# Relative products of pair 0 and loads of pairs 0 to 3 moved into layer 0's experts, router logits by token tile, part of layer 1's weight split moved into the softmax stage

## The chip, the cores and the metric

The kernel runs on one core of a Trainium2 chip. The metric is device time in microseconds (us), as the median of three runs. Engines are called PE (TensorE, matmul), PEld (its weight load), DVE (VectorE), ACT (ScalarE), POOL (GpSimd) and SP (SyncE). SPq and POOLq are the queues from which SP and POOL issue DMAs.

## The reference

Two transformer layers over x of shape (2, 1024, 128), 2048 tokens. Each layer is

```
xn = layernorm(x)
x  = x + attention(xn) + mixture_of_experts(xn)
```

- Layer 0, attention: 16 heads of 8, Q, K and V are xn with signs, probabilities are a causal sigmoid of the scores (no row maximum).
- Layer 0, experts: 32 experts of width 64, the top 4 of a softmax router with group limits, and a shared expert of width 128. In the kernel all experts are computed for all tokens and weighted, most weights being zero.
- Layer 1, attention: q, k, v and output projections, softmax, 16 heads of 8, and a relative term: the score of query i and key j has an added product of q_i with one of 256 position vectors, chosen by the offset of j from i and constant outside a band.
- Layer 1, experts: 16 experts of width 176, the top 4 of a sigmoid router, and a shared expert of width 352, weighted likewise.

## The kernel before

Everything is one program of five stages, each a block with a body for every engine. An engine runs its body in the order written; all engines meet between two blocks. Semaphores written by hand order the rest.

1. `prepare` and `sigmoid_attention` (to 210 us): layer 0's attention, with the split of layer 0's expert weights beside it.
2. `experts` with k = 0 (212 to 403 us). Matrix products in this kernel are three matmuls each: an operand is a high part (`_hi`, rounded) and a low part (`_lo`, the rest), and hi x hi, lo x hi and hi x lo are summed. The 2048 tokens are 4 tiles `ti` of 512 columns, the hidden rows 17 chunks of 128, so K = 17 and M = 68 steps n. In step n, PE does `rise(n)` (gate and up products, 6 matmuls) and `fall(n-2)` (down product, 3 matmuls); ACT the silu and the high part of the hidden chunk; DVE the product with gate, then with `share`, the expert weights of each token (L1499); POOL the low part. The tile `share` has four slots (WB = 4): in its step n, SP waits until the hidden chunk n-4 is done and issues the loads of share n (L234, one per expert in the chunk, so two as a rule).
   After the last chunk of a tile, its finish follows in the steps behind it, beside the next tile's chunks: `after(n)` gives the tile and the offset o. At o = 3 to 13 the tile is turned, added to x and normalized, at 13 to 14 turned back and split, at 16, 18 and 20 PE makes q, k and v of layer 1. All these go through one PSUM bank, `z_ps`, so that each waits until the one before is copied out: q is split at o = 17, k at 19, v is saved at 21. SP stores q (three DMAs, L1198) at o = 21 and k (six DMAs, `ka` and `kb`, L1203) at o = 23. For the last tile the same offsets run behind the last chunk (TAIL = 24).
3. `softmax_attention` (403 to 932 us): 16 pairs of heads, each with 16 slots. `scores(m)` (L885) gives the scores from which DVE takes row maxima; LS = 14 slots later `turned(n)` (L898) computes them again with keys on the partitions, for the exponential (L977), and `values` multiplies them with v (L925). The relative products `offsets(r)` (L872), 384 wide, are saved by ACT (L973), stored by SP with a padded row to DRAM (L773) and read back skewed (L786), two to a read; DVE adds them in the band (L1022), PE in the turned scores (L910). They lead by LR = 26 slots, so that the stage opens with 12 slots in which only relative products are made; there they use the free PSUM banks and DVE helps to save them (L1010). The loads of pair 0 are SP's (L762), those of pairs 1 to 3 POOL's (L816), behind the fills of `qs`, `ka` and `kb` (L800, L990, L991). At the stage's start PE computes the router's logits for all 16 token tiles (L931 to L933); DVE's `choose` picks experts between slots. Every eight slots PE turns the eight columns of row maxima (L956), DVE copies them (L1042), and SP stores them into `qs`. Behind the last slot the router's weights are turned (L279), copied by ACT (L288) and stored by SP (L294). POOL stores every finished half pair of the output (L826).
4. `experts` with k = 1 (932 to 1193 us): the same loop with K = 25 and M = 100. No weights are ready; groups of three chunks are loaded by SP into `raw` (L1159, L1162), split by ACT (L1327) and POOL (L1231) while the first tile runs. Before the loop SP also loads the attention output and its sums, `xn` and `v`, 1 MB each (L1187).

Of the kernel before, what the change touches and what calls it, by code (L numbers as in the profile page):

```python
# [54 lines left out]
LO_ROW = 64  # L55
SHARES = 4
# [40 lines left out]
def choose(router, sb, dve, then, chosen, part):  # L97
# [80 lines left out]
    else:  # L178
# [8 lines left out]
        dve.tensor_tensor(cw[:, :, 0:E], hot[:, 0], view(rs[:, 1, :], [1, NT], [0, E]), ALU.mult).then_inc(router.cw_ready, 1)  # L187

# [258 lines left out]
def sigmoid_attention(nc, d, sb, scr, router, weights, y_stored):  # L447
# [7 lines left out]
    KEPT = 10  # L455
    HELD, LAG = 9, 4
    TURN, STEP = 20, 6 * P
    UPPER, LOWER = (0, 7, 1, 6, 2, 5, 3, 4), (0, 3, 1, 2)
    with ExitStack() as ctx:
# [6 lines left out]
        qs, ks = tile("q", [P, 2, T], F32R), tile("k", [P, 2, T], F32R)  # L466
# [196 lines left out]
def softmax_attention(nc, d, sb, scr, router, weights, y_stored, table):  # L663
# [3 lines left out]
    KEYROWS = 31  # L667
# [7 lines left out]
    KEPT = 6  # L675
    VALUES = (2, 1, 0, 2, 0, 2, 0, 1, 1, 2, 1, 0, 2, 0, 2, 0)
    KEYS = ((5, 0, 1, 6, 2, 7, 3, 4), (4, 0, 3, 5, 1, 6, 2, 7))
    with ExitStack() as ctx:
# [31 lines left out]
        rel_ready, saved_act, saved_dve = sem("rel_ready"), sem("saved_act"), sem("saved_dve")  # L710
# [8 lines left out]
        def rows(pair, hd, count):  # L719
            g = 2 * (pair % 2) + hd  # L720
            return slice(32 * g, 32 * g + count)
# [4 lines left out]
        LEAD = LR - LS  # L726

        def on_act(r):
            return r >= LEAD or r % 2 == 0

        def rel_bank(r):
            if r >= LEAD or r % 5 == 0:
                return rel_ps
            return duo[1 + r % 5 // 3][:, r % 5 % 2 * CH:(r % 5 % 2 + 1) * CH]

        def saved_before(r):
            return sum(on_act(x) for x in range(r)), sum(not on_act(x) for x in range(r))

        slots = range(-LR, SLOTS + 4)
        job_of = {}  # L740
        for n in slots:
# [107 lines left out]
        def _(pe):  # L849
# [86 lines left out]
            for n in slots:  # L936
# [3 lines left out]
                if r < SLOTS:  # L940
                    offsets(r)
# [696 lines left out]
```

## Time and profile before

| what | value |
|---|---|
| three runs | 1195.48, 1197.96, 1201.27 us |
| median | 1197.96 us |
| profiled execution | 1194.37 us |
| its span, first to last instruction | 1192.6 us |
| busy, share of the span | PE 86%, PEld 54%, DVE 63%, ACT 61%, POOL 45% |
| mean granted clock of PE | 0.947 of full speed |
| DMA | 197.42 MB, mean 166 GB/s |

The profile is one execution. The busy shares are means over stages that differ; where PE is not busy at nine tenths or more, the page's slices and the windows show it. Times within the profile count from the start of the span.

### The profile page before, as it was taken

The page shows a single profiled execution, that of the slowest core. Times are in us where ns is not written, and L with a number is a line of the kernel's source. Part 1 is how long each engine was busy: PE and PEld are TensorE (multiplying, and loading weights), DVE is VectorE, ACT ScalarE, POOL GpSimd, SP SyncE. Part 2 cuts the span into 40 slices and gives each one's busy share as a digit, 9 for nine tenths or more (in the row PEclk, how much of TensorE's full clock was granted, in tenths as well). Part 3 has the DMA queues.
Part 4 walks back from the last instruction along what each step waited for, and adds up shares of the span by engine and source line. Part 5 has one row for each costly group of instructions (what it writes and reads, how often), then busy time and mean ns, then how long its engine had stood idle before and what let it go on. Part 6 is the DMA issues. An engine that isn't in the chain of part 4 may idle for free. (4 is left out here: it accounts for less than half of the span.)

```text
span 1192.6 us, 22324 instructions
## 1 busy us (share of the span) xinstructions
PE 1026.4 (86%) x7844; PEld 648.4 (54%) x7844; DVE 755.5 (63%) x1671; ACT 729.6 (61%) x1096; POOL 540.1 (45%) x723
## 2 busy tenths in 40 slices
PE   1499999999996548999999999999998178999997
PEld 1344444777774524554555555455544156878785
DVE  6145241677876247787788888777771056676766
ACT  1289988555553126777777777777765065555453
POOL 1166776465553130444434333333223187655554
PEclk9999999999998557999999999999999599999999
DMA  5521231644563297888888888888740554433443
GB/s 132 227 85 53 64 119 45 150 121 137 164 187 107 98 257 246 246 239 242 243 238 242 241 243 238 244 244 243 224 139 11 169 168 120 124 116 121 116 122 94
DMA packets 147132, 197.42 MB, mean 166 GB/s; under 512 B 34361, under 2 KB 113562, under 8 KB 146970
## 3 DMA queue, kind: packets, MB, share of 16 engines
q1 hardware_dynamic: 125868, 184.98, 50.8%
q0 software_dynamic: 21152, 11.01, 5.6%
q8 instruction: 62, 1.02, 0.4%
q14 instruction: 50, 0.41, 0.1%
HBM read 123.00 MB, written 72.74 MB: 164 GB/s over the span
## 5 line engine op out<-in xcount | busy, mean ns | idle before, releaser
L977 ACT ACTIVATE a_probs<-a_duo 128x1024 f32<-128x1024 f32 x256 | 261.7, 1025 | 80.5 <-PE a_duo L910 79.6
L1376 POOL TENSOR_TENSOR f_hid_lo<-f_hid,f_hid_hi 128x512 fp32r<-128x512 f32 (+1 forms) x168 | 216.6, 1291 | 147.6 <-ACT f_hid_hi L1347 147.6
L826 POOL DMA_DIRECT2D scr_y1c<-ys x256 | 126.7, 504 | 252.4 <-DVE ys L1005 240.1
L1029 DVE TENSOR_REDUCE a_part<-a_duo 128x2 f32<-128x1024 f32 (+3 forms) x256 | 215.5, 855 | 12.2 <-PE a_duo L885 10.8
L1022 DVE CUSTOM_DVE_ANT_0 a_band_sum<-a_duo,a_rel_raw 128x256 f32<-128x256 f32 (+2 forms) x320 | 131.4, 448 | 87.8 <-PE a_duo L885 58.2
L973 ACT ACTIVATE a_rel<-a_rel_ps 128x384 f32<-128x384 f32 x246 | 120.3, 489 | 55.4 <-PE a_rel_ps L872 39.3
L636 ACT ACTIVATE a_probs<-a_duo 128x1024 f32<-128x1024 f32 x192 | 139.7, 830 | 21.5 <-PE a_duo L585 20.1
L925 PE MATMUL a_acc_ps<-a_probs,a_v 128*32 128x256 f32 x2048 | 143.7, 387 | 0.1
L872 PE MATMUL a_rel_ps<-emb_all,a_q 31*128 31x384 f32 x247 | 112.8, 457 | 28.9 <-ACT a_rel L973 11.6
L574 POOL TENSOR_TENSOR a_probs<-a_probs,const 128x256 f32<-128x256 f32 x128 | 100.1, 798 | 58.4 <-ACT a_probs L636 58.1
L1495 DVE TENSOR_TENSOR f_u<-f_u,f_gate 128x512 f32<-128x512 f32 (+1 forms) x100 | 69.7, 697 | 86.6 <-PE f_u L1250 45.5
L1342 ACT ACTIVATE f_gate<-f_g 128x512 f32<-128x512 f32 (+1 forms) x100 | 59.7, 597 | 93.3 <-PE f_g L1246 93.3
L1347 ACT ACTIVATE f_hid_hi<-f_hid 128x512 fp32r<-128x512 f32 (+1 forms) x168 | 104.9, 624 | 18.8 <-DVE f_hid L1499 18.4
L910 PE MATMUL a_duo<-const,a_rel_raw 128*128 128x128 f32 x704 | 113.1, 287 | 0.0
L872 PEld LDWEIGHTS a_rel_ps<-emb_all,a_q 31*128 31x128 f32 x247 | 46.8, 189 | 112.0 <-issue 64.2
L898 PE MATMUL a_duo<-a_q,a_ka 32*128 32x512 f32 (+3 forms) x416 | 96.7, 409 | 1.4 <-DVE a_part L1029 0.4
L885 PE MATMUL a_duo<-a_ka,a_q 31*128 31x512 f32 (+3 forms) x416 | 97.5, 438 | 0.4 <-DVE a_rows L1042 0.4
L606 PE MATMUL a_acc<-a_probs,a_v 128*32 128x256 f32 (+1 forms) x1280 | 97.2, 369 | 0.2
L910 PEld LDWEIGHTS a_duo<-const,a_rel_raw 128*128 128x128 f32 x704 | 74.8, 141 | 34.0 <-issue 26.9
L1342 ACT ACTIVATE f_gate<-f_g,w_b 128x512 f32<-128x512 f32 x68 | 46.8, 688 | 63.9 <-PE f_g L1246 63.9
L585 PE MATMUL a_duo<-a_q,a_k 24*128 24x512 f32 (+3 forms) x384 | 67.2, 415 | 16.9 <-DMA a_k<-scr_k 14.9
L1499 DVE TENSOR_TENSOR f_hid<-f_u,f_share 128x512 f32<-128x512 f32 (+1 forms) x100 | 69.2, 692 | 17.3 <-POOL f_hid_lo L1376 4.8
(235 smaller groups left out, 1932.5 us busy)
## 6 DMA issues: line engine op xcount, KB each, us to landing
scr_rel<-a_rel SPq DMA_DIRECT2D x128, 384.0 KB, 3.8
a_rel_raw<-scr_rel SPq DMA_DIRECT2D x128, 384.0 KB, 4.5
w_share<-scr_cw SPq DMA_DIRECT2D x128, 128.0 KB, 3.2
f_share<-scr_cw SPq DMA_DIRECT2D x40, 256.0 KB, 3.2
scr_y1c<-ys POOLq DMA_DIRECT2D x256, 8.0 KB, 3.7
f_raw<-in_w SPq DMA_DIRECT2D x21, 192.0 KB, 3.3
f_share<-scr_cw SPq DMA_DIRECT2D x20, 192.0 KB, 2.9
f_share<-scr_cw SPq DMA_DIRECT2D x16, 224.0 KB, 3.0
```

The source lines that it names most:

```text
L636: act.activation(probs[:, n % KEPT, :, lo:HALF], duo[n % 3][:, :, lo:HALF], ACT.Sigmoid, scale=SCALE).then_inc(sig_done, 1)
L826: pool.dma_start(scr["y1c"][w, b, head, :, at:at + QUARTER], ys[32 * (2 * hd + c) + HD * w:32 * (2 * hd + c) + HD * (w + 1), h % 2, :]).th ...
L872: pe.matmul(rel_bank(r)[:, 0:BAND], qs[to, home(pair), j * P:(j + 1) * P], emb_all[to, :], start=True, stop=True).then_inc(rel_ready, 1)
L910: ins = pe.matmul(out[:, at:at + P], rel_raw[:, (8 * pair + j) % RING, hd, c:c + P], ident, is_transpose=True, start=False, stop=True, ski ...
L925: ins = pe.matmul(acc[to:to + 32, 0:QUARTER], vs[:, pair % 2, hd, kt, :], probs[:, n % KEPT, at:at + QUARTER], start=(n % 8 == 0), stop=(n ...
L973: act.activation(rel_sb[:, e % 4, r % 2, :], rel_bank(r)[:, 0:BAND], ACT.Copy).then_inc(saved_act, 1)
L977: act.activation(probs[:, n % KEPT, :], bank_pair("t", n)[:], ACT.Exp, scale=SCALE).then_inc(exp_done, 1)
L1022: ins = dve.tensor_tensor_reduce(band_sum[:, m % 2, hd, 0:wide], both[:, hd, (a - 4 * x) * P:(b - 4 * x) * P], rel_raw[:, e % RING, hd, (a ...
L1029: ins = dve.tensor_reduce(part[:, h % 2, x, :, j % 4], both[:, :, lo * P:hi * P], AX.X, ALU.max, negate=True)
L1342: act.activation(gate[0:m, n % 2, :], g_ps[n % 2][0:m, :], ACT.Silu, **bias).then_inc(gate_ready, 1)
L1347: act.activation(hid_hi[0:m, (n - 1) % 4, :], hid[0:m, (n - 1) % 2, :], ACT.Copy).then_inc(hi_ready, 1)
L1376: pool.tensor_tensor(hid_lo[0:m, n % 4, :], hid[0:m, n % 2, :], f32(hid_hi[0:m, n % 4, :]), ALU.subtract).then_inc(lo_ready, 1)
```

## The change

What it does:

- Layer 1's tiles `qs`, `ka`, `kb` live from the start in one buffer, `sb["att"]`. POOL fills it in steps 6 to 16 of layer 0's experts. The buffer takes room: the sigmoid stage keeps 8 probability tiles, not 10, and starts its values at slot 7, not 9; the softmax stage's probability tiles lie partly in `xn` and `yT`; layer 1's `hid_hi`, `y_hi` and `y_lo` lie in `att`.
- In layer 0's experts SP issues all 24 loads of pairs 0 to 3: two in each of the steps 54 to 56 (pair 0), one in each of the steps 57 to 74. PE makes pair 0's 16 relative products in steps 58 to 73 (into `y_ps[0]`), ACT saves each a step later into one of three slots, SP stores it a step after that.
- The offsets of the tile's finish are named and moved (table `MID`): q at 15 and split at 15, q stored at 16, k at 17 and split at 17, k stored at 18, v at 19, and new, the logits of this tile's four token tiles at 20. For the last tile (`END`) the offsets are shorter and each step has a PSUM bank of its own.
- The softmax stage begins with `scores(0)`: no fills, no loads of pairs 0 to 3, no lead of relative products, no logits. SP reads back the eight relative pieces of pair 0 at once.
- In the last eight half pairs before the end, two token tiles of router weights are turned together with the row maxima (`joint`, 72 columns); nothing of it is left behind the last slot. SP, not POOL, stores the last two half pairs, the last one in the next stage, and issues the first four shares of layer 1.
- POOL loads and splits the weights of layer 1's first 7 chunks (3 pieces) during pairs 8 to 10 in its own loop's counting of the softmax stage. Layer 1's experts start with them; the loading and splitting of groups of three begins with chunk 7.

```diff
@@ experts
-    TAIL = 24 if k == 0 else 8
+    TAIL = 22 if k == 0 else 4
+    MID = {"finish": 3, "turn": 5, "residual": 6, "centre": 7, "square": 8, "variance": 9, "scale": 11, "turn_norm": 13, "x_parts": 13,
+           "q": 15, "q_parts": 15, "q_store": 16, "k": 17, "k_parts": 17, "k_store": 18, "v": 19, "v_save": 19, "logits": 20, "logits_save": 20}
+    END = {"finish": 1, "turn": 2, "residual": 2, "centre": 3, "square": 4, "variance": 5, "scale": 6, "turn_norm": 7, "x_parts": 7,
+           "q": 8, "q_parts": 8, "q_store": 8, "k": 9, "k_parts": 9, "k_store": 9, "v": 10, "v_save": 10, "logits": 11, "logits_save": 11}
+        def bank(name, ti):
+            if ti < NC - 1:
+                return z_ps
+            return {"turn": u_ps[1], "turn_norm": u_ps[2], "q": g_ps[0], "k": g_ps[1], "v": u_ps[0], "logits": y_ps[1]}[name]
+        FILL, LOAD, REL = 6, 3 * K + 3, 3 * K + 7
@@ SP, in the loop over n (the share loads stay ahead of this)
-                    if k == 0 and o == 21:
+                    if k == 0 and name == "q_store":
                         sp.wait_ge(q_lo_ready, ti + 1)
...
-                    if k == 0 and o == 23:
+                    if k == 0 and name == "k_store":
                         sp.wait_ge(k_lo_ready, 2 * ti + 2)
...
+                if k == 0 and n == LOAD:
+                    sp.wait_ge(ahead.filled, 6)
+                    sp.wait_ge(q_stored, 96)
+                    sp.wait_ge(k_stored, 192)
+                if k == 0 and n >= LOAD:
+                    for pair, name, dst, hd in (first[2 * (n - LOAD):2 * (n - LOAD) + 2] if n < LOAD + 3 else first[n - LOAD + 3:n - LOAD + 4]):
+                        sp.dma_start(f32(dst[head_rows(pair, hd, TERMS * HD), pair // 2, :]), scr[name][:, 2 * pair + hd]).then_inc(ahead.rest_loaded if pair else ahead.first_loaded, 16)
+                r = n - REL - 2
+                if k == 0 and 0 <= r < AHEAD:
+                    sp.wait_ge(ahead.rel_saved, r + 1)
+                    sp.dma_start(scr["rel"][r // 2, r % 2, :, P - 1:P - 1 + BAND], emb[:, r % 3, :]).then_inc(ahead.rel_stored[r % 3], 16)
@@ PE, at the end of step n
+            def offsets(r):
+                if r == 0:
+                    pe.wait_ge(ahead.first_loaded, 96)
+                    pe.wait_ge(y_ready, NC - 1)
+                    pe.wait_ge(table_ready, 1)
+                wait(pe, ahead.rel_saved, r)
+                to, j = head_rows(0, r % 2, KEYROWS), r // 2
+                pe.matmul(y_ps[0][:, 0:BAND], qs[to, 0, j * P:(j + 1) * P], table["emb_all"][to, :], start=True, stop=True).then_inc(ahead.rel_ready, 1)
+                if k == 0 and 0 <= n - REL < AHEAD:
+                    offsets(n - REL)
@@ ACT, step n, between the silu and the high part
+                r = n - REL - 1
+                if k == 0 and 0 <= r < AHEAD:
+                    act.wait_ge(ahead.rel_ready, r + 1)
+                    wait(act, ahead.rel_stored[r % 3], 16 * (r // 3))
+                    act.activation(emb[:, r % 3, :], y_ps[0][:, 0:BAND], ACT.Copy).then_inc(ahead.rel_saved, 1)
@@ softmax_attention
-        slots = range(-LR, SLOTS + 4)
+        slots = range(-LS, SLOTS + 4)
@@ SP, before the slots
-            sp.wait_ge(ones_ready, 3)
-            for name, dst in (("q1h", qs), ("kah", ka), ("kbh", kb)):
-                for hd in range(2):
-                    sp.dma_start(f32(dst[rows(0, hd, K3), home(0), :]), scr[name][:, hd]).then_inc(first_loaded, 16)
+            for s in range(3):
+                sp.wait_ge(ahead.rel_stored[s], 16 * len(range(s, AHEAD, 3)))
+            for e in range(AHEAD // 2):
+                read(e)
@@ SP, behind the slots
-            weights_stored(router, sb, scr, sp)
+            sp.wait_ge(router.cw_saved, NB)
+            for i in range(2):
+                sp.dma_start(scr["cw"]...).then_inc(router.cw_stored, 16)
+            y_store(sb, scr, sp, y_saved, 2 * PAIRS - 2, y_stored[2])
+            sp.wait_ge(router.cw_stored, 32)
+            for n in range(SHARES):
+                share_out(weights, scr, sp, weights.share, n)
@@ POOL, in its loop over pair = 4 .. PAIRS + 3
+                if pair >= 8:
+                    for _ in range(2 if pair == 8 else 1):
+                        next(loading, None)
+                    for _ in range(2):
+                        next(splitting, None)
@@ experts with k = 1, SP, before its loop
             if k == 1:
+                y_store(sb, scr, sp, None, B * H - 1, y_stored[2])
                 sp.dma_start(wp[:], d["wproj"]).then_inc(small, 16)
@@ two_layers
-        weights = Weights(nc, ctx, L1, 0, False)
+        weights = Weights(nc, ctx, L1, 7, True)
```

## Rows read from the trace of the kernel before

**Rows 1.** The page's 40 slices of the span: TensorE's granted clock in tenths.

```profile
PEclk9999999999998557999999999999999599999999
```

**Rows 2.** Windows: from:to, length, busy time (instructions) of each engine, clock, DMA, GB/s.

```profile
240.00:270.00 30.00, 30.00 (x131) 23.76 (x130) 21.73 (x32) 16.29 (x28) 17.80 (x14) 1.00 0.42 122
403.00:418.00 15.00, 10.38 (x48) 10.32 (x48) 4.38 (x4) 1.70 (x2) 3.11 (x5) 0.50 0.11 40
416.00:417.00 1.00, 0.00 (x0) 0.00 (x0) 0.00 (x0) 0.00 (x0) 0.00 (x0) 0.50 0.20 82
500.00:800.00 300.00, 282.17 (x2817) 150.73 (x2809) 241.52 (x722) 232.13 (x329) 118.56 (x236) 1.00 0.85 242
943.00:956.00 13.00, 0.12 (x1) 0.00 (x0) 0.00 (x0) 2.82 (x5) 1.43 (x2) 0.62 0.75 267
```

**Rows 3.** Timeline, last tile of layer 0's experts: start, duration, instruction, idle before.

```profile
372.96 0.50 PE L1266 MATMUL f_y<-f_hid_lo,w_w_hi 128*128 128x512 f32 x1 [0.63 <-POOL f_hid_lo L1376]
...
376.83 0.68 DVE L1397 TENSOR_TENSOR yT<-f_y,f_yv 128x512 f32<-128x512 f32 x1
...
388.80 0.60 ACT L1351 ACTIVATE x_hi<-f_z 128x512 fp32r<-128x512 f32 x1 [13.33 <-PE f_z L1285]
...
396.21 1.41 DVE L1456 SCALAR_TENSOR_TENSOR f_k_lo<-f_z,f_ecol,f_k_hi 128x512 fp32r<-128x512 f32 x2 [3.04 <-ACT f_k_hi L1360]
...
403.61 1.80 POOL L800 MEMSET a_ka<- 128x2048 f32 x1 [16.74 <-POOLq L1059]
```

**Rows 4.** Timeline, opening of the softmax stage.

```profile
408.04 1.55 SPq L762 DMA_DIRECT2D a_q<-scr_q  x2
...
418.42 0.68 PE L872 MATMUL a_rel_ps<-emb_all,a_q 31*128 31x384 f32 x1 [4.39 <-DMA a_kb<-scr_kb]
...
434.32 0.42 DVE L1022 CUSTOM_DVE_ANT_0 a_band_sum<-a_duo,a_rel_raw 128x256 f32<-128x256 f32 x1 [7.34 <-DMA a_rel_raw<-scr_rel]
...
449.74 0.27 DVE L1042 CAST a_rows<-a_rel_ps 8x128 fp32r<-8x128 f32 x1
...
455.70 0.62 PE L898 MATMUL a_duo<-a_q,a_kb 32*128 32x512 f32 x2
```

**Rows 5.** Timeline, layer 0's experts: SP's queue around one tile's stores, then one step.

```profile
333.54 0.58 SPq L1198 DMA_DIRECT2D scr_q<-f_q_hi  x1
...
335.14 3.16 SPq L234 DMA_DIRECT2D w_share<-scr_cw  x4
338.65 0.80 SPq L1203 DMA_DIRECT2D scr_ka<-f_k_hi  x2
...
342.09 7.54 SPq L234 DMA_DIRECT2D w_share<-scr_cw  x8
...
365.57 0.39 PE L1244 MATMUL f_g<-x_hi,w_w_hi 128*128 128x512 f32 x1
...
368.16 0.69 DVE L1499 TENSOR_TENSOR f_hid<-f_u,w_share 128x512 f32<-128x512 f32 x1
```

**Rows 6.** Tile w_share, 333 to 350 us: from issue to landing.

```profile
DMA to landing us min/median/max: 3.3/4.1/4.9
```

**Rows 7.** Timeline: first matmul behind the exit of the sigmoid stage.

```profile
211.88 0.47 PE L1244 MATMUL f_g<-x_hi,w_w_hi 128*128 128x512 f32 x1 [2.32 <-PEq L459]
```

**Rows 8.** Timeline, end of the softmax stage and start of layer 1's experts.

```profile
917.71 0.42 DVE L1005 COPY ys<-a_acc_ps 128x256 f32<-128x256 f32 x1 [9.10 <-PE a_acc_ps L925]
...
918.42 3.95 POOL L826 DMA_DIRECT2D scr_y1c<-ys  x8 [5.43 <-DVE ys L1005]
...
932.55 0.84 SPq L1162 DMA_DIRECT2D f_raw<-in_w  x2
...
939.76 0.47 SPq L1187 DMA_DIRECT2D v<-scr_y1c  x1
...
953.15 1.35 ACT L1327 ACTIVATE f_w_hi<-f_raw 128x384 fp32r<-128x384 f32 x3 [15.04 <-DMA f_raw<-in_w]
...
966.98 0.69 DVE L1499 TENSOR_TENSOR f_hid<-f_u,f_share 128x512 f32<-128x512 f32 x1
```

More of the change, by code:

```diff
@@ L464, in sem @@
             return ctx.enter_context(nc.semaphore("a0_" + name))
-        qs, ks = tile("q", [P, 2, T], F32R), tile("k", [P, 2, T], F32R)
+        qs, ks = (sb["att"][:, i, :, :] for i in range(2))
         vs = tile("v", [P, 2, 2, NB, 32])
@@ L660, in _, with y_store, softmax_attention @@
                 next(beside, None)
-def softmax_attention(nc, d, sb, scr, router, weights, y_stored, table):
+def y_store(sb, scr, eng, saved, h, done):
+    pair, x = h // 2, h % 2
+    if saved is not None:
+        eng.wait_ge(saved, h + 1)
+    for hd in range(2):
+        for c in range(2):
+            b, head = pair // (H // 2), 2 * pair % H + hd
+            at = x * (T // 2) + c * (T // 4)
+            for w in range(2):
+                eng.dma_start(scr["y1c"][w, b, head, :, at:at + T // 4],
+                              sb["ys"][32 * (2 * hd + c) + HD * w:32 * (2 * hd + c) + HD * (w + 1), h % 2, :]).then_inc(done, 16)
+def softmax_attention(nc, d, sb, scr, router, weights, y_stored, ahead, table):
     SCALE = HD ** -0.5
     K3 = TERMS * HD
-    KEYROWS = 31
     MROW = KEYROWS
@@ L717, in wait @@
                 eng.wait_ge(s, value)
-        def rows(pair, hd, count):
-            g = 2 * (pair % 2) + hd
-            return slice(32 * g, 32 * g + count)
+        rows = head_rows
         def home(pair):
             return pair // 2 % 2
[L726 to L737, printed above, removed]
-        slots = range(-LR, SLOTS + 4)
+        slots = range(-LS, SLOTS + 4)
         job_of = {}
@@ L783, in _ @@
                         sp.wait_ge(st_ready, 16 * pair + j // 4 * 8 + last + 1)
[L784 to L786 removed]
+                    read(e)
                 m = n + LS - 3
@@ L1046, in _, with experts @@
                 pass
-def experts(nc, d, sb, scr, layer, weights, y_stored, y_counts, table=None):
+def experts(nc, d, sb, scr, layer, weights, y_stored, y_counts, ahead, table=None):
     k = layer.index
@@ L1300, in project_v, with logits @@
                 return ins
+            def logits(ti):
+                for t in range(4 * ti, 4 * ti + 4):
+                    out, cols = bank("logits", ti)[:, (t % 4) * L1.E:(t % 4 + 1) * L1.E], slice(t * P, (t + 1) * P)
+                    pe.matmul(out, x_hi[:, cols], table["gw_hi"][:], start=True, stop=False)
+                    pe.matmul(out, x_lo[:, cols], table["gw_hi"][:], start=False, stop=False)
+                    ins = pe.matmul(out, x_hi[:, cols], table["gw_lo"][:], start=False, stop=True)
+                return ins
+            def offsets(r):
+                if r == 0:
+                    pe.wait_ge(ahead.first_loaded, 96)
+                    pe.wait_ge(y_ready, NC - 1)
[3 more added lines that the diff above has]
+                pe.matmul(y_ps[0][:, 0:BAND], qs[to, 0, j * P:(j + 1) * P], table["emb_all"][to, :], start=True, stop=True).then_inc(ahead.rel_ready, 1)
             for n in range(M + TAIL):
```

318 lines of the change are left out of this document (164 added, 154 removed).

## The prediction

> **What bounds the kernel now.** I read the page's slices of PE's clock first [rows 1]: it is at its upper level (2.4 GHz) except in three places, slices 13 to 16 (358 to 477 us) and slice 32 (924 to 954 us), where it falls to 0.5 (1.2 GHz). Next come the windows by stage [rows 2]. In layer 0's experts (240 to 270) PE is busy all the time: 131 matmuls, nine to a step, give 2.06 us a step. In the body of the softmax stage (500 to 800) PE has 282 of 300 us. From 943 to 956 PE has one matmul. So PE bounds the long stretches, and the time that is not PE's lies at the two seams.
>
> The first seam [rows 3, 4]: the last hidden chunk ends at about 373.3, the last tile's finish starts at 376.83, and its dependent steps run to 403.61, when the next stage starts. Fills, then six loads from 408.04, then the first relative product at 418.42; the first band sum waits for its read until 434.32; the first turned slot is at 455.70. That is 52.1 us from the stage's start to its first useful exponential. The second seam [rows 8]: the last values are copied at 917.71, POOL's stores are issued until 922.4, SP starts only at 932.55, the raw weights queued behind the 1 MB load at 939.76 come at 953.15, and the hidden product of the fifth chunk is at 966.98, 34.4 us behind the stage's first DMA.
>
> **The change part by part**, against the profiled execution (1194.4 us: span 1192.6 and 1.8 around it; it is 0.3% under the median).
>
> *Opening of the softmax stage: -30.1.* Fills, loads and lead are gone. SP issues eight reads at once; a read took 16 engines' time, by the steady 242 GB/s [rows 2] 1.6 us for its 393 KB. The first lands about 3.5 us in, the next faster than DVE uses them (two slots each). Then DVE is the chain: between 434.32 and 455.70 it worked through 13 slots, 21.4 us, of which I take off 2.7 us of waits for late reads: 18.7. So the first turned slot comes at 3.5 + 18.7 = 22 us, not 52.1. Bounds: 18 (DVE starts at once) and 30 (the reads crowd as they did before 434).
>
> *Tail of layer 0's experts: -2.2.* The finish need not wait behind k's split (376.83 against 373.3), but DVE's order now puts tile 2's v and logits between the steps of tile 3, and the ring of three slots for relative pieces turns over only as its stores land. I follow SP there: six k stores, then a load and a store a step, each piece 4 us to land, so that the last is saved near 387 or 388 and the split of x starts at 388.0, for 388.80. From there each bank of its own saves the wait of k for q's split (0.69 and an issue, 1.4 us with its hand-over): 0.8 + 1.4 = 2.2. The tail's cover is SP; bounds -8 (only DVE's chain) and +4.
>
> *Added PE work in layer 0: +4.3.* Logits: 48 matmuls took 10.38 us at the lower clock [rows 2], 0.216 each, so 0.108 at the upper; 24 of them (tiles 0 and 1) lie in PE's full stretch: 2.6. Relative products: ten lie beside chunks, 384 columns against 512 in 0.229 us (2.06 / 9), 0.17 each: 1.7. ACT's save of 0.49 fits into its idle time, POOL's six fills of 0.9 us (half of the 1.80 in [rows 3]) likewise. The removed logits were hidden by the loads anyway.
>
> *SP's queue in layer 0: +15, the largest cost.* The shares have four slots, and SP issues them in order with the tile's stores. Within a step the rise starts at t, the hidden product, which needs the share, at t + 2.6 (the last two of [rows 5]), ending at t + 3.3. So SP's step n begins at t(n) - 5.0. Before, a tile's q was split at offset 17 and stored at 21, k at 19 and 23: four steps between, and SP never waited; its gap from 338.65 to 342.09 is only the six issues, 3.4 us. Now the distance is one step, and in SP's order that means it waits for an event about three steps ahead. q is ready at t + 4.35 (2.06 for the step's nine matmuls, 0.69 for q's three, a copy of 0.60, a subtraction of 0.69, hand-overs 0.3); its three issues take 1.6 (333.54 to 335.14 in [rows 5]); the share of two steps on is issued from t + 5.95, its second half at 6.55, and lands 3.7 us later (3.3 to 4.9 [rows 6]): t + 10.2. It is wanted at 2.76 + 2.06 + 2.6 = t + 7.4. Late 2.8. For k, DVE can split only behind the late hidden product: done at t' + 7.2 (two subtractions, 1.41 [rows 3]), issues until 10.6, the share lands at 11.2 + 4.1 = 15.3 against 7.4: late 7.9 in all. PE has 0.4 us of slack, so 7.5 a tile, and 15 for tiles 0 and 1 (tile 2's stores come behind the last shares). Bounds: 0, if the prefetch covers it, and 20. PE also idles twice a tile, and its clock may fall: +2 (0 to 8).
>
> *Loads and stores beside the last tile: +7.* While SP's six loads were in flight, DMA had a share of 0.20 of 16 engines, 82 GB/s [rows 2], window 416 to 417: three engines busy and thirteen idle, though several loads were queued. One load of 96 KB thus holds the same three for some 1.25 us. In steps 54 to 67 these engines carry 17 loads (21), 14 pairs of shares (0.42 of a step, 0.9 us each: 12.2) and 8 relative stores (half of a steady pair of read and store, 0.7 each: 5.6), 39 us, for 14 steps of 2.06 and the 1.7 above: 30.5. With the wait for k's stores to land before the first load (share 55 is behind it), less the prefetch's slack: 7. Bounds 0 and 14.
>
> The Trainium skill says why ("DMA: Bandwidth & Descriptors", "Why a DMA increments its semaphore by 16 and not by 1"): the number of engines is the largest up to 16 that divides the slowest dimension of both sides, here 3 and 24, so 3; those issued by SP take the lowest-numbered ones, while those issued by POOL rotate. By that rule moving 18 loads from POOL to SP is a loss in itself, and the trace agrees with three engines; were the loads spread over sixteen, this term would be some 5 us less.
>
> *Softmax body: +3.* Eight half pairs get a copy into `joint`, its wait, and a copy out (0.27 at 449.74 in [rows 4]): 0.6 us each at most on the way from row maxima to PE, 4.8 in all; I take 3 with POOL's splits, which lie in its idle time (118.6 busy of 300 [rows 2]). Bounds 0 and 8.
>
> *Exit and start of layer 1's experts: -21.7.* POOL has no DMA in the last 15 us, nothing is turned or stored behind the last slot. An exit without such work took PE 2.3 us [rows 7], so PE restarts at 919.8, not at a stage start of 932.5: -12.7. Chunks 0 to 6 are ready, so 0 to 3 run at once. But share 4 stands in SP's queue behind six raw issues (2.8), eight stores (8 x 0.45), their landing (3) and the two 1 MB loads: the v load is issued 9.7 us in (7.2 before), the next weights land 13.4 us after that (939.76 to 953.15 [rows 8]), share 4 a microsecond later, and PE restarts at the lower clock (1.5): fifth hidden product at 25.5, not 34.4. -9.0. From there four splits of three chunks remain on either side. Bounds -14 and -4; 0 to +2 for the exit if it does not shrink.
>
> Sum: 4.3 + 15 + 2 + 7 - 2.2 - 30.1 + 3 - 21.7 = -22.7. The profiled time becomes 1171.7; it lay 0.3% under the median before, and I take half of that: **1173 us**.
>
> **The rivals.**
>
> A. *SP's lead suffices.* The prefetch of four shares covers waits and crowding, layer 0 loses only its 4.3 and some 3. For it: before, 7.54 us of queued share loads from 342.09 on in [rows 5] were caught up without a gap in PE. Against it: then SP reached the store after its data was ready. Time 1173 - 21 = 1152.
>
> B. *The exit keeps its 12.7 us*, because it is not POOL's DMAs that hold it but the stage's end as such. For it: nothing in the trace names what SP waited for from 922.4 to 932.5. Against it: 2.3 at the exit without DMAs of POOL [rows 7]. Time 1173 + 12 = 1185.
>
> C. *The opening is limited by DMA*: eight reads and the rest of the traffic come as slowly as between 418 and 434, and the lead that was cut had been hiding them. First turned slot at 40 us: 1173 + 18 = 1191, within noise of before. Against it: before 434, 18 loads of POOL were in flight too.
>
> D. *Slower: PE's clock stays low in layer 0.* Place: steps 33 to 67. Each late share is a gap of PE of 2 to 7 us, and before 403 the clock was at 0.5 from such a thin stretch [rows 1, 2]. A step at the lower clock takes nine matmuls of 0.43, 3.9 us, so +1.8; over 35 steps 62, less some 15 of stalls that this hides: 1220. It decides from 12 steps more at the low clock than I allow (21 / 1.8). Against it: from 966 on PE has gaps of 1 to 2 us every 8, and those slices are at 9 [rows 1].
>
> **How the numbers follow.** A measurement tells some 0.5% from no change. My case (1160 to 1183) 0.52; A 0.20; B 0.13; C 0.07; D 0.05; the rest, 0.03, below 1145. The range 1150 to 1191 leaves out the better half of A, the upper part of C, and D, 0.2 together. Faster by over 0.5% (under 1192): mine, A, B and half of C: 0.88; within 0.5%: 0.05; slower: 0.07.
>
> **What would show it.** Right: hidden products of steps 34, 36, 51 and 53 waiting for a DMA of w_share, 2 to 5 us each; SP idle ahead of L1198's and L1203's successors; a first turned slot 20 to 24 us behind the stage's start; PE back within 3 us at the second exit, and a gap of about 12 us before the fifth hidden product. Wrong: the softmax stage starting before 415 (A), a gap of over 8 us at the second exit (B), DVE waiting for a_rel_raw in the opening (C), a granted clock of 0.5 in layer 0's experts outside the tail (D).

## The result, and the profile after

The changed kernel takes 1162.45 us (median of four executions, 1159.57 to 1164.43) against 1199.11 us for the kernel before (four, 1195.48 to 1201.27). The ratio is 0.9695, 95% interval 0.9661 to 0.9729: 3.1% faster. The forecast was 1173, 10.5 us too high, with 1162 inside the range. Of the executions behind the times below, three stand apart and are in the medians but not in the ratios: 4505.0 us of e1, 1162.3 of e5, and 2266.1 of the kernel before that ran beside e5 to e8. The profiled execution took 1161.4 us (span 1159.6) against 1194.4 (span 1192.6), 33.0 us less, where the sum said 22.7.

Both spans cut at five marks that exist in either trace (start of an instruction, us; changes are of the unrounded times):

| stretch | before | after | change | forecast |
|---|---|---|---|---|
| start to the last hidden product of layer 0 | 370.2 | 395.6 | +25.4 | +28.3 |
| from there to the first instruction of the softmax stage | 33.4 | 32.6 | -0.8 | -2.2 |
| from there to the first turned slot | 52.1 | 22.1 | -30.0 | -30.1 |
| from there to the last copied values | 462.0 | 466.9 | +4.8 | +3 |
| from there to the fifth hidden product of layer 1 | 49.3 | 19.7 | -29.6 | -21.7 |
| from there to the end | 225.6 | 222.7 | -2.9 | 0 |

The profile page of the changed kernel, its PE row and granted clock, to be held against [rows 1]:

```profile
PE   1499999999898957999999999999999889999997
PEclk9999999999898955999999999999999999999999
```

The dip that was in slices 13 to 16 is now in 15 and 16 (slices of 29.0 us, so 406 to 464 us), shallow ones have come up in 11 and 13 (290 to 319, 348 to 377), and the one at slice 32 is gone. Windows of the changed kernel, columns as in [rows 2]:

```profile
300.00:330.00 30.00, 25.12 (x99) 19.82 (x100) 19.53 (x31) 11.96 (x19) 12.99 (x11) 0.83 0.48 117
330.00:360.00 30.00, 23.93 (x109) 18.86 (x108) 16.45 (x24) 12.36 (x20) 11.33 (x9) 0.94 0.53 151
```

From 300 to 360 PE has 208 matmuls, where at the 131 in 30 us of [rows 2] it would have 262, and the clock is at 0.83 and 0.94. The timeline of layer 0's experts shows why (start, duration, instruction, and in brackets the idle time before it and what ended it):

```profile
288.44 2.39 SPq L253 DMA_DIRECT2D w_share<-scr_cw  x4
292.88 0.69 DVE L1571 TENSOR_TENSOR f_hid<-f_u,w_share 128x512 f32<-128x512 f32 x1 [2.82 <-DMA w_share<-scr_cw]
294.92 0.80 SPq L1226 DMA_DIRECT2D scr_ka<-f_k_hi  x2
299.10 6.22 SPq L253 DMA_DIRECT2D w_share<-scr_cw  x10
303.34 0.69 DVE L1571 TENSOR_TENSOR f_hid<-f_u,w_share 128x512 f32<-128x512 f32 x1 [6.29 <-DMA w_share<-scr_cw]
...
345.27 0.69 DVE L1571 TENSOR_TENSOR f_hid<-f_u,w_share 128x512 f32<-128x512 f32 x1 [3.71 <-DMA w_share<-scr_cw]
355.90 0.69 DVE L1571 TENSOR_TENSOR f_hid<-f_u,w_share 128x512 f32<-128x512 f32 x1 [6.47 <-DMA w_share<-scr_cw]
...
395.62 0.69 DVE L1571 TENSOR_TENSOR f_hid<-f_u,w_share 128x512 f32<-128x512 f32 x1
```

The four rows of L1571 that wait for w_share are the hidden products of steps 34, 36, 51 and 53: 2.82, 6.29, 3.71 and 6.47 us, 19.3 in all. At 288.44 SP issues shares, has nothing more to issue until k's split is done, starts the k stores at 294.92 and comes to the next share at 299.10.

Opening of the softmax stage in the changed kernel, to be held against [rows 4]:

```profile
428.19 0.15 POOL L827 MEMSET a_part<- 128x64 f32 x1 [16.56 <-POOLq L1064]
431.50 0.42 DVE L1015 CUSTOM_DVE_ANT_0 a_band_sum<-a_duo,a_rel_raw 128x256 f32<-128x256 f32 x1 [0.73 <-DMA a_rel_raw<-scr_rel]
450.30 0.62 PE L908 MATMUL a_duo<-att 32*128 32x512 f32 x2
```

The first band sum comes 3.3 us behind the stage's start, the first turned slot 22.1 us behind it. The end of that stage and the start of the next, against [rows 8]:

```profile
917.15 0.42 DVE L1003 COPY ys<-a_acc_ps 128x256 f32<-128x256 f32 x1 [9.09 <-PE a_acc_ps L935]
917.85 0.83 SPq L1184 DMA_DIRECT2D f_raw<-in_w  x2
917.89 0.47 PE L1278 MATMUL f_g<-x_hi,w_w_hi 128*128 128x512 f32 x1 [0.81 <-PEq L711]
926.83 0.47 SPq L1210 DMA_DIRECT2D v<-scr_y1c  x1
936.82 0.69 DVE L1571 TENSOR_TENSOR f_hid<-f_u,w_share 128x512 f32<-128x512 f32 x1 [3.14 <-DMA w_share<-scr_cw]
```

PE's first matmul is 0.74 us behind the start of the last copy; before, SP came back 14.8 us behind it.

### The profile page after: what moved, and what is told of

It reads as the page before. It is cut to its first block and busy times, and to the rows that moved or that the text cites. A ratio compares the mean times of both kernels' runs of the same rounds, so it can differ in the third digit from the quotient of the medians.

```text
span 1159.6 us, 22263 instructions
## 1 busy us (share of the span) xinstructions
PE 1035.2 (89%) x7828; PEld 652.0 (56%) x7828; DVE 753.9 (65%) x1682; ACT 728.6 (63%) x1087; POOL 535.7 (46%) x692
## 5 line engine op out<-in xcount | busy, mean ns | idle before, releaser
L1022 DVE TENSOR_REDUCE a_part<-a_duo 128x2 f32<-128x1024 f32 (+3 forms) x256 | 215.5, 855 | 13.5 <-PE a_duo L895 11.9
L1442 POOL TENSOR_TENSOR f_hid_lo<-f_hid,att 128x512 fp32r<-128x512 f32 (+1 forms) x100 | 129.6, 1297 | 104.5 <-ACT att L1413 104.2
L655 ACT ACTIVATE a_probs<-a_duo 128x1024 f32<-128x1024 f32 x192 | 139.8, 828 | 21.6 <-PE a_duo L604 20.1
L895 PE MATMUL a_duo<-att 31*128 31x512 f32 (+3 forms) x672 | 145.0, 427 | 8.7 <-DVE a_part L1022 4.0
L908 PE MATMUL a_duo<-att 32*128 32x512 f32 (+3 forms) x672 | 137.9, 408 | 14.9 <-DVE a_part L1022 12.7
L1571 DVE TENSOR_TENSOR f_hid<-f_u,w_share 128x512 f32<-128x512 f32 (+1 forms) x168 | 116.2, 692 | 50.3 <-DMA w_share<-scr_cw 29.2
L1442 POOL TENSOR_TENSOR f_hid_lo<-f_hid,f_hid_hi 128x512 fp32r<-128x512 f32 x68 | 88.1, 1296 | 89.1 <-ACT f_hid_hi L1413 89.0
L882 PE MATMUL a_rel_ps<-emb_all,att 31*128 31x384 f32 x240 | 108.5, 452 | 10.9 <-DVE a_rows L1040 9.0
L979 ACT ACTIVATE yT<-a_duo 128x1024 f32<-128x1024 f32 x86 | 88.0, 1025 | 28.0 <-PE a_duo L920 27.6
L979 ACT ACTIVATE xn<-a_duo 128x1024 f32<-128x1024 f32 x86 | 88.0, 1025 | 26.9 <-PE a_duo L920 26.3
L979 ACT ACTIVATE a_probs<-a_duo 128x1024 f32<-128x1024 f32 x84 | 86.0, 1025 | 27.5 <-PE a_duo L920 27.1
L1567 DVE TENSOR_TENSOR f_u<-f_u,f_gate 128x512 f32<-128x512 f32 (+1 forms) x100 | 69.7, 697 | 49.3 <-PE f_u L1284 43.2
L908 PEld LDWEIGHTS a_duo<-att 32*128 32x128 f32 x672 | 64.1, 184 | 48.7 <-DVE a_part L1022 32.3
```

The lines of the kernel that those rows point to most:

```text
L655: act.activation(probs[:, n % KEPT, :, lo:HALF], duo[n % 3][:, :, lo:HALF], ACT.Sigmoid, scale=SCALE).then_inc(sig_done, 1)
L882: pe.matmul(rel_ps[:, 0:BAND], qs[to, home(pair), j * P:(j + 1) * P], emb_all[to, :], start=True, stop=True).then_inc(rel_ready, 1)
L895: ins = pe.matmul(out[:, at + a * P:at + b * P], qs[to, home(pair), j * P:(j + 1) * P], kv[to, home(pair), a * P:b * P], start=True, stop= ...
L908: ins = pe.matmul(out[:, at + a * P:at + b * P], kv[to, home(pair), kt * P:(kt + 1) * P], qs[to, home(pair), a * P:b * P], start=True, sto ...
L979: act.activation(probs[n % KEPT], bank_pair("t", n)[:], ACT.Exp, scale=SCALE).then_inc(exp_done, 1)
L1022: ins = dve.tensor_reduce(part[:, h % 2, x, :, j % 4], both[:, :, lo * P:hi * P], AX.X, ALU.max, negate=True)
```

## The experiments

Each kernel ran beside the kernel before on the same chip; the ratios are to that.

| kernel | us | ratio, 95% |
|---|---|---|
| changed | 1162.5 | 0.9695 (0.9661 to 0.9729) |
| e1 late stores | 1148.2 | 0.9563 (0.9523 to 0.9603) |
| e1 again | 1151.2 | 0.9618 (0.9573 to 0.9662) |
| e2 late q store | 1165.0 | 0.9722 (0.9685 to 0.9759) |
| e10 late k store | 1156.1 | 0.9651 (0.9606 to 0.9696) |
| e3 POOL stores the last half pairs | 1175.0 | 0.9807 (0.9776 to 0.9837) |
| e4 no chunk split early | 1176.4 | 0.9829 (0.9791 to 0.9867) |
| e5 uniform rows (on e1) | 1152.0 | 0.9615 (0.9587 to 0.9643) |
| e5 again | 1145.9 | 0.9574 (0.9526 to 0.9623) |
| e6 1 MB loads later (on e1) | 1156.0 | 0.9638 (0.9609 to 0.9667) |
| e7 shares first (on e1) | 1146.9 | 0.9568 (0.9540 to 0.9596) |
| e9 = e1 + e5 + e7 | 1144.7 | 0.9550 (0.9518 to 0.9582) |
| e8 before, early stores | 1212.6 | 1.0129 (1.0098 to 1.0160) |

The experiments ran in three groups (e1 to e4; e5 to e8; e9, e10 and the two repeats), each on one chip, so that ratios and not times compare across groups. Single executions of one kernel spread over up to 13 us (e1 again: 1144.8 to 1157.9), so that a few us are settled by the traces and not by these times.

**e1: q and k stored later.**

```
-  "q_store": 16, ... "k_store": 18,
+  "q_store": 19, ... "k_store": 21,
-  FILL, LOAD, REL = 6, 3 * K + 3, 3 * K + 7
+  FILL, LOAD, REL = 6, 3 * K + 4, 3 * K + 8
```

> The changed kernel, with SP's q store at offset 19 instead of 16 and k store at 21 instead of 18 (the loads of pairs 0 to 3 and the relative products start one step later, since they wait for k's stores). Theory (SP's queue: the four waits of hidden products for w_share, 2.8 + 6.3 in tile 0 and 3.7 + 6.5 in tile 1, come from shares queued behind stores that SP reached too early): these waits vanish, PE's clock between 300 and 370 stays at 1.0, the softmax stage starts some 20 us earlier (near 408), time near 1144 (1140 to 1150). Rival (layer 0 is longer because of the added PE work and of DMA crowding by loads and relative pieces, the share waits being only where it shows): the waits move to other steps, time 1156 to 1164.

Measured: 1148.2, within the expected 1140 to 1150. The waits of steps 34, 36, 51 and 53 are gone, the clock from 300 to 380 is 1.0, the last hidden product starts at 379.9 instead of 395.6 (-15.7) and the stage at 411.9 instead of 428.2. What is left in layer 0 is three smaller waits, in steps 56 to 58, beside the loads:

```profile
348.44 0.69 DVE L1571 TENSOR_TENSOR f_hid<-f_u,w_share 128x512 f32<-128x512 f32 x1 [1.15 <-DMA w_share<-scr_cw]
352.17 0.69 DVE L1571 TENSOR_TENSOR f_hid<-f_u,w_share 128x512 f32<-128x512 f32 x1 [2.37 <-DMA w_share<-scr_cw]
356.62 0.69 DVE L1571 TENSOR_TENSOR f_hid<-f_u,w_share 128x512 f32<-128x512 f32 x1 [1.65 <-DMA w_share<-scr_cw]
```

The rival falls. The theory's 20 us for the stage's start came out as 16.3, for these three waits (5.2 us) are new: the changed kernel has 0.25 us there. Its loads pass where PE is held up anyway, so a stall that goes uncovers the next.

**e2 and e10: only q, only k stored later.** e2 has `"q_store": 19` alone; e10 has `"k_store": 21` and LOAD and REL as in e1.

> The changed kernel with q stored at offset 19 instead of 16, so now behind k's store at 18; k's store stays early. Theory: the wait of 2.8 to 3.7 us for the share two steps behind the q store goes in each of tiles 0 and 1, the wait of 6.3 to 6.5 behind k's store shrinks only by what it owed to the late hidden product before it (to some 4 or 5): 8 to 10 us off, time near 1153. Rival (one late step simply absorbs the other; only the later one sets the pace): 0 to 3 us off, 1159 to 1162.

> The changed kernel with k stored at offset 21 instead of 18 and q's store left at 16 (loads and relative products one step later, as in e1). With e1 and e2 it completes the four combinations. Theory as in the prediction (the q store costs 2.8 to 3.7 us of its own in each of tiles 0 and 1, the k store 5 to 6): the late k alone brings half of e1's gain or a little more, 1152 to 1156. Rival after e2 (the two are not a sum: k's store alone costs 7 to 8 us a tile whether q's is early or not, and q's wait is absorbed by it): with k late, q's wait remains in full and is 2.8 to 3.7 us a tile, 6 us above e1: 1153 to 1155; the discriminating number is in the trace: whether any wait but q's is left in layer 0.

Measured: e2 1165.0, no gain at all; e10 1156.1, just above the expected 1152 to 1156. The hidden products that wait for a share in layer 0, e2:

```profile
300.75 0.69 DVE L1571 TENSOR_TENSOR f_hid<-f_u,w_share 128x512 f32<-128x512 f32 x1 [5.89 <-DMA w_share<-scr_cw]
304.98 0.69 DVE L1571 TENSOR_TENSOR f_hid<-f_u,w_share 128x512 f32<-128x512 f32 x1 [2.27 <-DMA w_share<-scr_cw]
349.43 0.69 DVE L1571 TENSOR_TENSOR f_hid<-f_u,w_share 128x512 f32<-128x512 f32 x1 [5.33 <-DMA w_share<-scr_cw]
353.35 0.69 DVE L1571 TENSOR_TENSOR f_hid<-f_u,w_share 128x512 f32<-128x512 f32 x1 [1.97 <-DMA w_share<-scr_cw]
```

With q late and k early the waits are 8.2 us in tile 0 (steps 36 and 37) and 7.3 in tile 1 (53, 54), against 9.1 and 10.2 with both early; further waits beside the loads (steps 55 to 57, 7.0 us) take up the rest. e10:

```profile
292.90 0.69 DVE L1571 TENSOR_TENSOR f_hid<-f_u,w_share 128x512 f32<-128x512 f32 x1 [2.89 <-DMA w_share<-scr_cw]
305.87 0.69 DVE L1571 TENSOR_TENSOR f_hid<-f_u,w_share 128x512 f32<-128x512 f32 x1 [0.60 <-DMA w_share<-scr_cw]
335.62 0.69 DVE L1571 TENSOR_TENSOR f_hid<-f_u,w_share 128x512 f32<-128x512 f32 x1 [2.88 <-DMA w_share<-scr_cw]
353.15 0.69 DVE L1571 TENSOR_TENSOR f_hid<-f_u,w_share 128x512 f32<-128x512 f32 x1 [5.16 <-DMA w_share<-scr_cw]
```

With k late q's wait stays at 2.9 in both tiles, and the loads find it tighter (8.4 us in steps 56 to 58). So in tile 0 k alone costs 8.2 us, q alone 3.5 (with 0.6 in step 39) and both 9.1, less than their sum; in tile 1 it is 7.3, 2.9 and 10.2, which is just their sum. In e2 the rival was right in the time, and half right in the reason. The waits behind the stores are 3.8 us shorter in all, but those beside the loads are 6.7 us longer. The last hidden product is 2.7 us earlier, the softmax stage 0.5. The 8 to 10 us of expected gain did not come.

**e3: the last two half pairs stored by POOL.**

```
-            y_store(sb, scr, sp, y_saved, 2 * PAIRS - 2, y_stored[2])    (SP, softmax stage)
-                y_store(sb, scr, sp, None, B * H - 1, y_stored[2])       (SP, layer 1's experts)
-                if pair < PAIRS + 3:                                     (POOL, twice)
-                    y_store(sb, scr, pool, ...)
+                y_store(sb, scr, pool, ...)
```

> The changed kernel with the last two half pairs of the output stored by POOL at the end of the softmax stage, as the kernel before did, instead of by SP, the second of them in the next stage. Everything else of the exit is as changed: no router weights are turned behind the last slot. Theory (the stage's end waits for POOL's own DMAs): PE restarts 10 to 14 us behind the last copied values instead of 0.8, time 1172 to 1176. Rival (the 15 us of the kernel before were the turning, saving and storing of router weights behind the last slot): PE restarts within 4 us, time 1162 to 1165.

Measured: 1175.0, as expected, 12.5 us more than the changed kernel.

```profile
916.16 4.08 POOL L692 DMA_DIRECT2D scr_y1c<-ys  x8 [5.37 <-DVE ys L1000]
930.07 0.76 PE L1274 MATMUL f_g<-x_hi,w_w_hi 128*128 128x512 f32 x1 [14.69 <-PEq L711]
```

POOL has issued its last store at 920.24, and PE comes back at 930.07 after 14.69 us of idling, though no router weights are handled behind the last slot. The theory holds: of the exit of the kernel before, POOL's own DMAs at the end are what costs, 9.8 us behind the last issue. The stores themselves have a median of 2.6 us from issue to landing. What the hardware waits for after that no row names.

e3 gives the last stores back to POOL and puts them back into the stage, both at once. That it is POOL's queue and not any late store is shown by the other exit of this kind, behind the sigmoid stage, in the kernel before. There SP issues eight such stores until 211.34, and PE's first matmul is at 211.88 [rows 7]:

```profile
207.97 3.37 SPq L523 DMA_DIRECT2D scr_y<-ys  x8
```

**e4: no chunk of layer 1 split early.**

```
-        weights = Weights(nc, ctx, L1, 7, True)
+        weights = Weights(nc, ctx, L1, 0, True)
```

> The changed kernel with no chunk of layer 1's weights loaded and split in the softmax stage (0 instead of 7); all 25 chunks are split in the experts stage in groups, as in the kernel before. The exit without POOL's stores and the early shares stay. Theory: the start of layer 1's experts gives back what the seven chunks were worth, some 10 us up to the fifth hidden product and 3 behind it, while the softmax body gets back 1 to 3 us of its 4.8: time 1169 to 1173. Rival (the weights split early are worth little, since share 4 stands behind the 1 MB loads in either case, and that is what ends last): 1160 to 1164.

Measured: 1176.4, 14 us more, and above the expected 1169 to 1173.

```profile
915.38 0.42 DVE L1003 COPY ys<-a_acc_ps 128x256 f32<-128x256 f32 x1 [9.10 <-PE a_acc_ps L935]
921.91 0.79 PE L1278 MATMUL f_g<-x_hi,f_w_hi 128*128 128x512 f32 x1 [6.60 <-POOL f_w_lo L1265]
946.45 0.69 DVE L1571 TENSOR_TENSOR f_hid<-f_u,w_share 128x512 f32<-128x512 f32 x1
```

The fifth hidden product is 31.1 us behind the last copy, against 19.7: 11.4 us, of 12.2 by which the two profiled spans differ. Behind it e4 takes 225.4 us to the end, against 222.7: 2.6 more. From the first turned slot to the last copy it takes 466.7 us (448.7 to 915.4), as the changed kernel does (466.9): POOL's loads and splits in the softmax stage cost nothing, and the expected 1 to 3 us did not come back.

**e5: 24 rows of one stride.** The scratch tensors of q, ka and kb are (B*H, 3, 8, T) instead of (3, B, 128, T), so that a load's source `scr[name][2 * pair + hd]` is 24 rows.

> e1 with the scratch copies of q, ka and kb laid out in DRAM so that the 24 rows of a head (3 parts of 8) follow each other at one stride; a load's source is then 24 rows where it was 3 blocks of 8. Same bytes. Theory (a load of 96 KB is carried by three DMA engines, which the shares and relative pieces also need, so that in e1 three hidden products wait 1.2, 2.4 and 1.6 us for their shares beside the loads, and the relative ring turns over slowly): by the rule of the Trainium skill (DMA: Bandwidth & Descriptors, why a DMA increments its semaphore by 16) the loads then take 12 engines, the three waits go, 4 to 7 us off in layer 0: near 1143. Rival (the waits come from SP's issue time, 0.75 us for a load against 0.38 for a share, with shares issued one by one behind it): the waits stay, 1146 to 1149.

> e5 once more, beside e1 on the same chip. If e5's first profiled execution (1142.3) was an outlier of a kernel that takes 1149 to 1154, this one is near 1150 and its trace shows where the 8 us lie that the first did not have; if the layout is as good as that trace says, 1141 to 1145.

Measured: 1152.0, and the second time 1145.9, beside 1151.2 for e1 on the same chip (ratios 0.9574 and 0.9618, whose intervals overlap): no difference that the times can tell. The first is above both ranges that were expected of it. The traces differ where they should. Windows from 345 to 360, first e1, then e5:

```profile
345.00:360.00 15.00, 12.72 (x52) 8.56 (x50) 8.95 (x15) 6.25 (x11) 6.39 (x5) 1.00 0.49 152
```

```profile
345.00:360.00 15.00, 15.00 (x65) 11.23 (x64) 12.42 (x20) 8.60 (x15) 8.41 (x8) 1.00 0.76 203
```

The waits for shares are down from 5.2 us to 0.4, PE is busy all the time, the DMA share is 0.76 instead of 0.49, and the last hidden product starts at 375.7, in the second trace at 377.0, against 379.9 and 380.2. The relative pieces land in 2.9 us instead of 4.7. In these traces the layout is worth 3 to 4 us up to that product. By the Trainium skill ("DMA: Bandwidth & Descriptors", "Why a DMA increments its semaphore by 16 and not by 1") a transfer takes the largest number of engines up to 16 that divides the slowest dimension of both sides, so 12 for 24 rows and 3 for three blocks of 8. The higher DMA share agrees with that, though no row counts engines.

**e6: the two 1 MB loads later.** The waits for the output's stores and the loads of xn and v stand in SP's loop at n == 7.

> e1 with the two loads of 1 MB of layer 1's experts (xn and v, wanted only from step 17 on) issued in step 7 of SP's loop instead of ahead of it, with the waits for the output's stores. Theory (the fifth hidden product waits 3.1 us for share 4, which stands behind those 2 MB and the stores they wait for): that wait goes, those of steps 7 to 12 grow a little where the 2 MB now pass; 2 to 5 us off, near 1144. Rival (the 2 MB cost the same wherever they pass, or share 4 is held by the raw load ahead of it, which waits for POOL's split until 929.8): 0 to 1 us off, 1147 to 1149.

Measured: 1156.0, no gain: its ratio of 0.9638 is above that of e1 (0.9563) and not clear of that of e1 again (0.9618). Share 4 gains 1 to 2 us of its wait (1.9, where e1 has 3.8 and 2.9), and the two shares next to the moved loads, issued from 933.31 on, pay (4.5 and 5.9):

```profile
929.19 0.69 DVE L1573 TENSOR_TENSOR f_hid<-f_u,w_share 128x512 f32<-128x512 f32 x1 [1.85 <-DMA w_share<-scr_cw]
939.75 0.69 DVE L1573 TENSOR_TENSOR f_hid<-f_u,w_share 128x512 f32<-128x512 f32 x1 [4.52 <-DMA w_share<-scr_cw]
947.39 0.69 DVE L1573 TENSOR_TENSOR f_hid<-f_u,w_share 128x512 f32<-128x512 f32 x1 [5.88 <-DMA w_share<-scr_cw]
```

Layer 1's waits for shares are 15.2 us in all, where e1 has 8.7 and 9.2. The time missed both ranges, but on share 4 the rival was right: SP takes up the raw load ahead of it 11.9 us behind the stage's first DMA, when POOL's split ends, in e6 (923.40) as in the changed kernel (929.77), with the 2 MB out of the way or not. That the 2 MB cost more in the loop, where shares have a lead of four steps and no more, is how I read the two long waits. Part of this profiled execution's length is not the edit's: its softmax stage took 475.0 us from the first turned slot to the last copy against 468.6 in e1, with one half pair of 17.4 us for 14.8.

**e7: shares ahead of the raw weights.**

```
+                if WB <= n < M: (wait for hid_ready, share_out)
-                if n in load_at: load(load_at[n])            (ahead of the shares)
+                if n - 1 in load_at: load(load_at[n - 1])    (behind them)
```

> e1 with SP's order in the experts changed: a step's shares ahead of the raw weights, and these one step later, so that no share stands behind a raw load that waits for POOL's split. Theory (the seven waits of layer 1's hidden products for w_share, 9.6 us in all, come each from such a raw load, whose wait for raw_lo was 15.8 us of SP's time in four): most of them go, 4 to 8 us off, near 1142. Rival (the raw weights become late instead, ACT and PE wait for f_raw and its split): no gain or up to 5 us slower, 1148 to 1153.

Measured: 1146.9, between the two ranges and with a ratio (0.9568) that is that of e1. In layer 1 the waits of hidden products for shares fall from 8.7 and 9.2 us in e1 to 3.0. From the last copied values to the end it takes 242.2 us all the same, against 243.1 and 241.6. ACT waits 5.0 us for raw weights instead of 3.0 and 3.2, as the rival had it in kind; what takes up the rest is not shown.

**e9: e1, e5 and e7 together; e1 again.**

> The late stores (e1), the 24 uniform rows (e5) and the shares ahead of the raw weights (e7) together. If the gain of e5's profiled execution (no waits for shares beside the loads, softmax stage 2.7 us earlier, body 2 us shorter) is real: 1141 to 1145. If e5's other runs tell the truth (1149 to 1154): 1148 to 1153, no better than e1.

> e1 once more, as the reference for e5_again, e9 and e10 on the same chip: 1144 to 1149, as in its first runs.

Measured: e9 1144.7, the lowest median, 1.5% better than the changed kernel by the ratios and steady (1142.4 to 1148.7), but by its interval not clear of e1, e5 again or e7; e1 again 1151.2, above its expected 1144 to 1149. Waits for shares in layer 0 of e9 (total, times, longest):

```profile
DVE f_hid L1571 <- DMA w_share<-scr_cw: 1.2, 2, 0.7
```

**e8: the kernel before with early stores.**

```
-                    if k == 0 and o == 21:      (q)
+                    if k == 0 and o == 18:
-                    if k == 0 and o == 23:      (k)
+                    if k == 0 and o == 20:
```

> The kernel before with only SP's stores moved: q's from offset 21 to 18 and k's from 23 to 20, each one step behind its split, which stay at 17 and 19. Nothing else of the change. Theory (distance between split and store is what SP's queue needs; no relative products, loads or logits in layer 0 are needed for the loss): hidden products of tiles 0 to 2's finishes wait for f_share, some 7 to 9 us a tile in three tiles, the softmax stage starts 20 us later and the time is near 1218 (1212 to 1224). Rival (the lateness in the changed kernel comes with the denser offsets of the splits, 15 and 17, and DVE's order): 1198 to 1203.

Measured: 1212.6, 13.5 us more than before and just inside the expected 1212 to 1224.

```profile
299.14 0.69 DVE L1499 TENSOR_TENSOR f_hid<-f_u,w_share 128x512 f32<-128x512 f32 x1 [3.21 <-DMA w_share<-scr_cw]
309.64 0.69 DVE L1499 TENSOR_TENSOR f_hid<-f_u,w_share 128x512 f32<-128x512 f32 x1 [3.72 <-DMA w_share<-scr_cw]
347.54 0.69 DVE L1499 TENSOR_TENSOR f_hid<-f_u,w_share 128x512 f32<-128x512 f32 x1 [3.59 <-DMA w_share<-scr_cw]
357.48 0.69 DVE L1499 TENSOR_TENSOR f_hid<-f_u,w_share 128x512 f32<-128x512 f32 x1 [2.63 <-DMA w_share<-scr_cw]
...
417.22 1.80 POOL L800 MEMSET a_ka<- 128x2048 f32 x1 [16.74 <-POOLq L1059]
```

Steps 36, 38, 53 and 55, each one step behind a store: 13.1 us in tiles 0 and 1. The stage starts at 417.22, 13.6 later than in [rows 3]. Nothing else of the change is in this kernel, so the loss is that of two offsets alone. The stage's start moved by less than the 20 us expected: the waits are 6.9 and 6.2 us a tile, not 7 to 9, and tile 2 has none, since its stores come behind the last shares.

## Why the forecast was right, point by point

The mechanisms of the forecast are all in the traces; what missed is sizes. Against the forecast, layer 0 came out 2.9 us shorter, the tail 1.4 longer, the opening to 0.1, the body 1.8 longer, the exit with layer 1's start 7.9 shorter and the rest 2.9 shorter. That is 10 us too little gain in all, most of it from one term, and the misses of the other terms cancel in part.

*SP's queue, +15 and +2 of clock.* Shown, to the step: the four waits stand where the forecast put them. Putting the stores back (e1) moves the last hidden product by 15.7 us, which holds the clock's part; e8 makes the same loss in the kernel before. Its inner division (2.8 for q, 5.1 more for k) fits the four waits, but not what each store costs by itself: k alone costs 8.2 of 9.1 us in tile 0 and 7.3 of 10.2 in tile 1.

*Added PE work, +4.3, and loads beside the last tile, +7.* The last hidden product starts at 370.2 before, at 375.7 to 377.0 where neither stores nor loads hold it (e5): 5.5 to 6.8. So the added work was put too low, and the loads, which cost 3 to 4 (e1 to e5) and not 7, too high. In the changed kernel the three terms cannot be added at full price, since the loads pass beside stalls: 25.4 in all, 28.3 forecast. That the sum came so near is in part luck.

*Tail, -2.2.* Measured -0.8.

*Opening, -30.1.* Measured -30.0. The read landed 3.3 us in, as forecast; DVE's chain took 18.8.

*Softmax body, +3.* Measured +4.8. Half pairs with `joint` take 14.8 us each where every second one took 14.2 before. The times of the copies, before and after:

```profile
825.55 0.41 DVE L1005 COPY ys<-a_acc_ps 128x256 f32<-128x256 f32 x1
839.73 0.41 DVE L1005 COPY ys<-a_acc_ps 128x256 f32<-128x256 f32 x1
854.49 0.41 DVE L1005 COPY ys<-a_acc_ps 128x256 f32<-128x256 f32 x1
```

```profile
823.30 0.41 DVE L1003 COPY ys<-a_acc_ps 128x256 f32<-128x256 f32 x1
838.05 0.41 DVE L1003 COPY ys<-a_acc_ps 128x256 f32<-128x256 f32 x1
852.90 0.42 DVE L1003 COPY ys<-a_acc_ps 128x256 f32<-128x256 f32 x1
```

Over the last eleven intervals that is 2.6 us, within the 3. Another 0.7 is spread over the twenty before. The last 1.5 lie between the first turned slot and the first copy and go with the clock: the same 158 matmuls were busy 18.1 us at a mean clock of 0.85 before and 20.2 at 0.72 after, so PE stayed at the lower clock for longer behind that slot. Why is not shown here.

*Exit and start of layer 1, -21.7.* Measured -29.6, and -2.9 behind it: this is the term that was mis-sized. The exit gave 14.1 (12.7 forecast); in e3, PE comes back 14.6 us behind the last copy, which gives 13.9 of it back. The fifth hidden product came 18.9 us behind PE's restart, not 25.5, so the start gave 15.5 (9.0 forecast). The failing step is "the next weights land 13.4 us after" the v load's issue. Times of the two 1 MB loads, issue to landing, before:

```profile
xn<-scr_y1c SPq DMA_DIRECT2D x1, 1024.0 KB, 10.2
v<-scr_y1c SPq DMA_DIRECT2D x1, 1024.0 KB, 11.7
```

and after:

```profile
xn<-scr_y1c SPq DMA_DIRECT2D x1, 1024.0 KB, 4.9
v<-scr_y1c SPq DMA_DIRECT2D x1, 1024.0 KB, 7.0
```

Before, six raw loads of 192 KB were issued right behind them (940.28 on), and all shared the engines. After, the 2 MB have a lead of 2.9 us: SP takes up the next raw load when POOL's split ends (926.83 to 929.75), and share 4 behind it.

```profile
929.77 0.84 SPq L1184 DMA_DIRECT2D f_raw<-in_w  x2
931.14 3.26 SPq L253 DMA_DIRECT2D w_share<-scr_cw  x6
```

The hidden product that waits for share 4 starts at 936.82, 10.0 us behind the v load's issue, where the forecast had 15.9 with the clock. I had taken a landing time from a queue with other company. But the 2 MB are not what holds share 4 here, as the forecast had it. In e6, where they are out of the way, its hidden product comes 17.7 us behind the stage's first DMA and not 19.0. Most of the wait is for SP to come to the share, and SP waits for POOL's split, which is not in the forecast's chain.

The last 2.9 had been set at nothing in the forecast ("four splits of three chunks remain on either side"). They belong to the chunks split early: e4, which splits none early, takes 225.4 us there, as the kernel before does (225.6).

*The rivals.* A (SP's lead suffices) and D (clock low for 35 steps) are refuted by the four waits and by clocks of 0.83 and 0.94. B (the exit keeps its time as such) is refuted by 0.74 us, by e3 and by the exit behind the sigmoid stage. C (opening limited by DMA) by the 22.1 us.

Open: what occupies the chip for 10 us behind POOL's last DMA; why single executions of e1, e5 and e6 differ by up to 13 us (the one half pair of e6 is a hint, no more); whether the relative products would be cheaper elsewhere in layer 0, which was not tried.

## What to carry to other kernels

When an in-order queue carries both prefetches and results, an item should reach its turn after its data is ready; three steps of an offset table moved the end of layer 0's experts by 14 to 16 us here (e8, e1). A landing time read from a row holds for the transfers that were in flight then: the load of v, 1 MB, took 7.0 us in one place and 12.7 in another. When a change takes neighbours away, ask as well what its issuer will wait for. And a stage that ended with POOL's stores ended about 14 us earlier when SP issued them, the last ones in the next stage.

## What was not expected of the hardware

POOL's last DMA issue held the end of a stage for 10 us more (920.24 to 930.07 in e3). Behind SP's last issue, at the end of the sigmoid stage, PE was back within 0.6 us (211.34 to 211.88). The two 1 MB loads took 4.9 and 7.0 us with a lead of 2.9 us on the next load, 10.2 and 11.7 with six loads of 192 KB right behind them, and 8.8 and 12.7 in e6, among shares and raw weights.
